# Row sums of one turn of an adjacency matrix: additions on GpSimd instead of sums on TensorE

## What is computed

```python
def _L0_gnn_ref(z, dist_matrix, W, B):
    msg = z @ W + B
    sens = exp(-(1.0 / r - 1.0 / MU) ** 2 / (2.0 * SIGMA * SIGMA))     # r = dist_matrix, MU 1, SIGMA 0.5
    weights = jnp.where(dist_matrix < CUTOFF, sens, 0.0)
    return weights @ msg

def _L1_gnn_ref(x, adj, W):
    A_hat = adj + jnp.eye(adj.shape[0], dtype=adj.dtype)
    d_inv_sqrt = jnp.sum(A_hat, axis=1) ** (-0.5)
    A_norm = d_inv_sqrt[:, None] * A_hat * d_inv_sqrt[None, :]
    support = x @ W.T
    return jax.nn.relu(A_norm @ support)

h = jnp.maximum(_layernorm(x, axis=-1), 0.0)
x = x + _L0_gnn_ref(h, adj, L0_gnn_W, L0_gnn_B)
h = jnp.maximum(_layernorm(x, axis=-1), 0.0)
x = x + _L1_gnn_ref(h, adj, L1_gnn_W)
```

## Time and profile before

| | |
|---|---|
| median of 3 runs | 580.74 us (579.77 to 583.24) |
| profiled execution | 580.75 us, its span 579.0 us |
| TensorE busy | 527.3 us (91%), granted clock 0.975 of full speed |
| DVE busy | 469.9 us (81%) |
| ACT busy | 462.3 us (80%) |
| GpSimd busy | 64.1 us (11%) |
| L443, the sums on TensorE | 256 instructions, 35.7 us |
| L697, the transposes on DVE | 64, 2303 ns each |
| L712, the cuts on DVE | 64, 2288 ns each |

### The profile page before, as it was taken

The page is one execution under the profiler, slowest core; times in us unless marked ns, Lnnn a source line. Parts: engine busy times, 40 slices in busy tenths (PEclk is TensorE's granted clock), DMA queues, the critical chain, the costliest instruction groups (busy, mean ns, idle before and its releaser), DMA issues.

```text
span 579.0 us, 4992 instructions
## 1 busy us (share of the span) xinstructions
PE 527.3 (91%) x1579; PEld 238.9 (41%) x1579; DVE 469.9 (81%) x556; ACT 462.3 (80%) x305; POOL 64.1 (11%) x100
## 2 busy tenths in 40 slices
PE   0658987989989999999999999999999999999995
PEld 0334423323333344344444444444444444445442
DVE  2999989999889896999999999995999559206244
ACT  1489999999899999898999989999699966920011
POOL 3993600000000000000000000000000001101000
PEclk9958998989999999999999999999999999999999
DMA  9999999999999997769979999998678040948223
GB/s 203 228 310 315 332 322 346 361 356 338 368 370 299 368 331 191 214 228 300 293 184 315 281 234 254 342 278 220 178 187 229 20 145 6 416 161 288 74 63 82
DMA packets 90652, 145.19 MB, mean 251 GB/s; under 512 B 10369, under 2 KB 81282, under 8 KB 81666
## 3 DMA queue, kind: packets, MB, share of 16 engines
q1 hardware_dynamic: 83088, 105.81, 64.8%
q0 software_dynamic: 5808, 38.28, 19.0%
q10 hardware_dynamic: 1730, 0.79, 0.7%
HBM read 106.04 MB, written 38.80 MB: 250 GB/s over the span
## 4 chain that ended last, share of the span: by engine, by line
PE 55%; ACT 26%; DVE 9%; issue 4%; DMA 3%; POOL 2%; ACTq 1%; DVEq 0%
PE acc L412 21%; PE mix L435 14%; PE mix L425 11%; ACT wt L568 7%; ACT wt L573 6%; ACT wt L587 5%; ACT wt L578 5%; DVE kept L697 3%; DMA x<-in_x_dram 3%; DVE rowpart L705 2%; PE mix L443 2%; PE acc L435 2%; POOL support L365 2%; DVE wt L712 2%; ACT wt L584 2%
## 5 line engine op out<-in xcount | busy, mean ns | idle before, releaser
L412 PE MATMUL acc<-wt,msg 128*128 128x512 f32 x512 | 237.5, 608 | 11.8 <-ACT wt L587 8.8
L412 PEld LDWEIGHTS acc<-wt,msg 128*128 128x128 f32 x512 | 96.0, 193 | 144.0 <-issue 118.4
L697 DVE STREAM_TRANSPOSE kept<-raw 128x2048 f32<-128x2048 f32 x64 | 147.4, 2303 | 2.5 <-DMA adj_t_spill<-kept 1.7
L712 DVE SCALAR_TENSOR_TENSOR wt<-kept 128x2048 f32<-128x2048 f32 x64 | 146.4, 2288 | 1.3
L568 ACT ACTIVATE wt<-wt 128x2048 f32<-128x2048 f32 x64 | 121.7, 1902 | 10.6 <-DVE wt L712 10.6
L573 ACT ACTIVATE wt<-wt 128x2048 f32<-128x2048 f32 x64 | 121.6, 1901 | 0.5
L425 PE MATMUL mix<-kept,support 128*128 128x512 f32 x224 | 101.1, 595 | 1.6 <-DVE kept L697 1.6
L587 ACT ACTIVATE wt<-wt 128x2048 f32<-128x2048 f32 x50 | 95.0, 1900 | 0.0
L578 ACT ACTIVATE wt<-wt 128x2048 f32<-128x2048 f32 x50 | 94.9, 1898 | 0.0
L435 PE MATMUL mix<-late,support 128*128 128x512 f32 x200 | 89.7, 593 | 0.0
L705 DVE TENSOR_REDUCE rowpart<-raw 128x16 f32<-128x4096 f32 x16 | 70.1, 4381 | 0.0
(11 more groups left out here) (93 smaller groups left out, 261.0 us busy)
## 6 DMA issues: line engine op xcount, KB each, us to landing
raw<-in_adj_dram SPq DMA_DIRECT2D x512, 128.0 KB, 6.2
adj_t_spill<-kept SPq DMA_DIRECT2D x35, 1024.0 KB, 10.6
late<-adj_t_spill POOLq DMA_DIRECT2D x26, 1024.0 KB, 8.6
raw<-adj_t_spill POOLq DMA_DIRECT2D x9, 1024.0 KB, 9.9
out_dram<-kept SPq DMA_DIRECT2D x30, 64.0 KB, 1.8
x<-in_x_dram POOLq DMA_DIRECT2D x24, 64.0 KB, 7.6
x<-in_x_dram ACTq DMA_DIRECT2D x8, 64.0 KB, 4.7
out_dram<-kept ACTq DMA_DIRECT2D x2, 64.0 KB, 2.1
```

What stands on the lines that cost most here:

```text
L412: mm = nc.tensor.matmul(acc0[:], msg[:, col(u) * T + k, :], wt[:, u % WTS, k, :], start=(first and k == 0), stop=(last and k == T - 1))
L697: nc.vector.transpose(dst, src).then_inc(turned, 1)
L712: nc.vector.scalar_tensor_tensor(out=wt[:, u % WTS], in0=v, scalar=CUTOFF, in1=v, op0=ALU.is_lt, op1=ALU.mult).then_inc(cut_done, 1)
```

## The change

In turn 3 TensorE no longer sums each unit. GpSimd adds the turned units up in `row_acc` (128x2048): the first addition takes units 24 and 25, each of the six others adds one more. TensorE sums the total with four products when all seven additions are done. `PE_SUMS` is 3 now, and `DVE_SUMS = 4` stands where `PE_SUMS` stood for the turns whose sums are DVE's. A transpose of the units 28 to 35 also waits for the addition that reads its slot. GpSimd's late loads are put between the additions by `load_unit`. For the 8 KB a partition that `row_acc` takes, the scratch of dynamic DMAs is set to 8192.

```diff
-PE_SUMS = 4
+PE_SUMS = 3
+DVE_SUMS = PE_SUMS + 1
+
+def added_by_pool(u):
+    return PE_SUMS <= u // G < DVE_SUMS
+
+def adds(u):
+    return max(1, u % G)

+def load_unit(j):
+    before = slot_before(j)
+    if before is None:
+        return G + 2 + j
+    return [u for u in sorted(JOBS) for _ in JOBS[u]][before] + 4

# GpSimd
+            def add(u):
+                pool.wait_ge(turned, u + 1)
+                if adds(u) >= 2:
+                    pool.wait_ge(pool_added, adds(u) - 1)
+                first = kept[:, (u - 1) % KEPT] if u % G == 1 else row_acc[:]
+                nc.gpsimd.tensor_tensor(row_acc[:].rearrange("p k i -> p (k i)"),
+                                        first.rearrange("p k i -> p (k i)"),
+                                        kept[:, u % KEPT].rearrange("p k i -> p (k i)"),
+                                        ALU.add).then_inc(pool_added, 1)
...
+            for u in range(G, UNITS):
+                for j in range(len(IN_TURN)):
+                    if load_unit(j) == u:
+                        load_late(j)
+                if added_by_pool(u) and u % G >= 1:
+                    add(u)
+            for j in range(len(IN_TURN), len(LOADED)):
+                load_late(j)

# TensorE
+            def sum_total():
+                pe.wait_ge(pool_added, G - 1)
+                for k in range(T):
+                    mm = nc.tensor.matmul(sum_bank[PE_SUMS][k * B:(k + 1) * B, :], ones[:], row_acc[:, k, :],
+                                          start=True, stop=True)
+                mm.then_inc(tiles_summed, 1)
...
                 if g >= 1 and idx < LAG:
                     multiply_weights(u - LAG)
-                if 1 <= g <= PE_SUMS and step_at(g, idx, "sum_quads"):
+                if u == DVE_SUMS * G:
+                    sum_total()
+                if 1 <= g <= DVE_SUMS and step_at(g, idx, "sum_quads"):
                     turn_sums(g - 1)

# ScalarE
-                act.wait_ge(tiles_summed, G * (g + 1))
+                act.wait_ge(tiles_summed, G * (g + 1) if g < PE_SUMS else G * PE_SUMS + 1)

# VectorE, in turn(u), with v = u - KEPT
+                    if added_by_pool(v):
+                        dve.wait_ge(pool_added, adds(v))

-    nc = _bacc.Bacc("TRN2", target_bir_lowering=False, num_devices=1)
+    nc = _bacc.Bacc("TRN2", target_bir_lowering=False, num_devices=1, dynamic_dma_scratch_size=8192)
```

More of the change, by code:

```diff
@@ L78 @@
 JOBS_FIRST = 4
-PE_SUMS = 4
+PE_SUMS = 3
[4 more added lines that the diff above has]
+    return max(1, u % G)
 def squared_by_dve(u):
-    return u < PE_SUMS * G and u % (4 if u < G else 2) == (3 if u < G else 1)
+    return u < DVE_SUMS * G and u % (4 if u < G else 2) == (3 if u < G else 1)
 STEPS = {"own_rows": (2, 3, 5), "copy_x1t": (1, 2, 6), "turn_x1": (2, 3, 5), "make_x1": (3, 4, 5),
@@ L167, in build @@
         wt = sb("wt", [P, WTS, T, ROWS])
+        row_acc = sb("row_acc", [P, T, ROWS])
         x1t = sb("x1t", [D, ROWS])
@@ L237, in build @@
         quad_done = sem("quad_done")
+        pool_added = sem("pool_added")
         tiles_summed = sem("tiles_summed")
@@ L296, in load @@
                 if n >= RAW:
-                    if n - RAW >= PE_SUMS * C4:
-                        sp.wait_ge(summed, n - RAW + 1 - PE_SUMS * C4)
+                    if n - RAW >= DVE_SUMS * C4:
+                        sp.wait_ge(summed, n - RAW + 1 - DVE_SUMS * C4)
                     sp.wait_ge(turned, 2 * (n - RAW + 1))
@@ L367, in _, with load_late @@
                 last.then_inc(h0_done, 1)
-            for j, (r, c) in enumerate(LOADED):
+            def add(u):
[7 more added lines that the diff above has]
+                                        ALU.add).then_inc(pool_added, 1)
+            def load_late(j):
+                r, c = LOADED[j]
                 slot = late_slot(j)
@@ L376, in _ @@
                     last_pair = max(n for n in range(PAIRS) if n % RAW == (slot - LATE) // 2)
[L377 removed]
+                    pool.wait_ge(summed, last_pair + 1 - DVE_SUMS * C4)
                     pool.wait_ge(turned, 2 * last_pair + 2)
@@ L454, in sum_quads @@
             def sum_quads(g):
-                pe.wait_ge(summed, C4 * (g + 1 - PE_SUMS))
-                if g == PE_SUMS:
+                pe.wait_ge(summed, C4 * (g + 1 - DVE_SUMS))
+                if g == DVE_SUMS:
                     pe.wait_ge(quad_stage, Q + 1)
@@ L493, in _ @@
                     multiply_msg(idx // 2)
-                if g > PE_SUMS and step_at(g, idx, "sum_quads"):
+                if g > DVE_SUMS and step_at(g, idx, "sum_quads"):
                     sum_quads(g - 1)
@@ L655, in _ @@
                     copy_h0((idx + 1) // 2)
-                if 1 <= g <= PE_SUMS and idx == 0:
+                if 1 <= g <= DVE_SUMS and idx == 0:
                     copy_sums(g - 1)
@@ L700, in row_sum @@
                 g, jp = n // C4, n % C4
-                if g >= PE_SUMS + 2 and jp == 0:
+                if g >= DVE_SUMS + 2 and jp == 0:
                     dve.wait_ge(quads_summed, g - 1)
@@ L768, in own_rows @@
                     dve.wait_ge(newton, 3 * g)
-                if g < PE_SUMS:
+                if g < DVE_SUMS:
                     nc.vector.tensor_copy(pows[:, 0, :], side[:, 0:T]).then_inc(rows_owned, 1)
@@ L798, in make_x1 @@
                 last.then_inc(hid_done, 1)
-                if g >= PE_SUMS:
-                    dve.wait_ge(rows_summed, g + 1 - PE_SUMS)
+                if g >= DVE_SUMS:
+                    dve.wait_ge(rows_summed, g + 1 - DVE_SUMS)
                 nc.vector.tensor_scalar(pows[:, 0, :], pows[:, 0, :], 1.0, None, ALU.add)
@@ L817, in turned_ahead @@
             def turned_ahead(u):
-                return u % 2 == 1 and u < PE_SUMS * G and squared_by_dve(u - 2)
+                return u % 2 == 1 and u < DVE_SUMS * G and squared_by_dve(u - 2)
             take_moments(0)
@@ L825, in _ @@
                     turn(u)
-                if g < PE_SUMS or u < PE_SUMS * G + 2:
+                if g < DVE_SUMS or u < DVE_SUMS * G + 2:
                     cut(u)
@@ L831, in _ @@
                         quad(u - 1)
-                if idx % 2 == 1 and g >= PE_SUMS:
+                if idx % 2 == 1 and g >= DVE_SUMS:
                     row_sum(u // 2)
@@ L841, in _ @@
                     make_support(g - 1)
-                if u >= PE_SUMS * G + 2:
+                if u >= DVE_SUMS * G + 2:
                     cut(u)
```

## The result

The changed kernel takes 596.18 us (median of 3 runs, 595.96 to 596.61) against 580.74 us before: ratio 1.0269, 95% interval 1.0245 to 1.0294, so 15.4 us slower. The forecast was 594.

What follows compares the result with a forecast made beforehand. DVE was taken as the chain up to 308 us, then TensorE. Additions of 4.5 us holding up DVE's two-operand passes sum to +13.6 us at T33: 580.75 + 13.6 = 594.4, 594 us; range 579 to 600.

Steps and rivals of the forecast that it cites:

- What bounds: DVE is the chain up to 308 us, then TensorE, so a shift of T33 is a shift of the end.
- T33: DVE's transpose of the unit numbered in the name, claimed to come at 260.6 instead of 247.00 us, +13.6.
- rival 4: Worse than 600 us, from additions above 5.5 us or a fall of TensorE's granted clock; chance 0.03.
- The additions' price: One GpSimd addition of 128x2048 float32 takes 4.5 us, between 3.9 and 5.5; seven are 31.5 us.
- Exclusion in both directions: Two-operand DVE passes and GpSimd's reads exclude each other; whichever holds the resource keeps it to the end of its instruction.
- Rivals 1 and 2: First: GpSimd yields to DVE, 580 us, chance 0.25. Second: additions hidden under transposes at no cost, 577.4 us, chance 0.08.
- Q23: DVE's square of unit 23, claimed to wait for the first addition and start at 192.7 instead of 188.76 us, +3.9.
- C29: DVE's cut of unit 29 in the fourth turn, claimed to be +10.7 us late.
- A29: GpSimd's addition for unit 29, claimed to run 231.7 to 236.2 us and hold small two-operand DVE passes behind C29.
- A31: GpSimd's addition for unit 31, claimed to hold DVE's cut of unit 32 to 256.2 instead of 241.47 us, +14.7.
- if GpSimd wins also between Q and C, +16: Case where GpSimd also gets in between DVE's square and cut: +16 us, 596.8 us.
- TensorE's gain, 3.3 us: Of 7.0 us of sums taken from TensorE, 3.3 us reach its product L478 and the DVE work behind it.

Runs made afterwards that it cites:

- e2: Changed kernel with all additions, DVE's cuts and squares of the fourth turn replaced by one-operand transposes of the same size: 577.62 us, ratio 0.9961 to the kernel before.
- e3: Changed kernel with each GpSimd addition replaced by three memsets, so GpSimd only writes: 578.19 us, ratio 0.9974 to the kernel before.
- e5: Changed kernel with each addition cut into four pieces of 512 columns: 584.41 us, ratio 1.0070 to the kernel before.
- e6: Changed kernel with each addition replaced by a GpSimd TENSOR_SCALAR reading one operand: 589.08 us, ratio 1.0144 to the kernel before.
- e4: Changed kernel with the additions kept and TensorE also summing each unit as before: 595.24 us, ratio 1.0266 to the kernel before.
- e9: Changed kernel with only the first three of seven additions, TensorE summing units 28 to 31 one by one: 584.48 us, ratio 1.0085 to the kernel before.
- e1: Changed kernel without GpSimd's additions, the total's buffer filled with ones once: 577.95 us, ratio 0.9969 to the kernel before.
- e7: Kernel before with only the scratch of dynamic DMAs set to 8192: 579.61 us, ratio 0.9985 to the kernel before.

## Why the prediction was right

**What bounds.** Right: DVE's T33 is 15.7 us late (262.39 against 247.00, and 0.3 for the axis) and the end is 15.4 us late. All of the loss arises between T25 and T33. TensorE's granted clock fell to 0.90 in the fourth turn, one of rival 4's conditions, but TensorE wasn't the chain there, and the time stayed under 600 us.

**The additions' price.** 4.54 us where 4.5 was taken, and 3.9 and 5.5 were the bounds. In e2, with nothing in the way, 4.55 to 4.58 us. The Trainium skill's 4.497 us for it (GPSIMD Engine Reference, Performance versus the Vector engine) is within 2% of that.

**Exclusion in both directions.** Right, and shown in both: the trace of after has DVE passes that wait for an addition and additions that wait for a DVE pass, e2 and e3 show that it takes DVE's two-operand passes (transposes of the same size aren't held) and GpSimd's reading, and e5 that the wait is as long as one instruction of the other side. Rivals 1 and 2 fall with Q23's 6.17 us. "To the end of the instruction" held for the additions, and not for e6's instruction.

**The sum.** Starts, with 0.3 us added for the axis of after:

| | forecast | measured |
|---|---|---|
| C25, behind Q23 | +3.9 | 194.56, +3.9 |
| C27 done, behind A27 | +8.6 | 214.4 against 206.7, +8.1 |
| C29's end | +10.7 | 235.1 against 221.1, +14.3 |
| T30 | +10.1 | 236.90, +9.2 |
| C31's end | +12.4 | 254.6 against 239.2, +15.7 |
| T33 | +13.6 | 262.39, +15.7 |

Up to T30 each term but C29's is within 0.9 us of the forecast. **One term was mis-sized**: A29 and A31. I had them start behind C29 and C31, and A31 half hidden beside T32. They got in between the square and the cut that follows it on DVE without a gap (C29 6.61 us, C31 6.60, each with a full 4.3 us of waiting in it). For A29 it made no difference, since it only changed which of DVE's passes waited. A31 was not beside a transpose at all: 3.3 us more at C31's end. C32, which I had held until 256.2, was then free of a hold, and the gap in front of Q31, which I had counted as gone, stayed (1.02 us). 15.7 against 13.6 is the whole error of the sum. The prediction had this order as the upper end of its own range ("if GpSimd wins also between Q and C, +16").

The total can be worked out in another way: DVE's passes are 23.0 us longer by the busy line, and it lost three waits, of 1.96, 0.19 and 5.10 us. 23.0 - 7.25 = 15.7 us. The same subtraction gives 15.8 for e4 (measured 15.4 by the ratio), 4.4 for e5, where 0.27 us of the first wait is left (4.1), 9.2 for e6 (8.4, with an interval from 5.7 to 11.0) and 5.5 for e9, where 3.09 of the 5.10 are left (4.9, from 3.0 to 6.9).

**TensorE's gain, 3.3 us.** Wrong in size, though the verdict didn't hang on it. The step that failed is "three of the five sums lie ahead of that product and give 1.3 us": I had looked at ACT's pass alone (it did come 1.4 us earlier in e1) and not at L466, which waits for DVE's L770. Before, L466 started 0.6 us behind L770's end (204.91 against 204.35), so it had little to gain. In e1 it stands for 2.6 us and the product behind it pays 1.35 us by its clock. The removal was worth 1.8 us.

**ACT and TensorE have time over, the kept slots, the late loads, the scratch.** Right: e4, e2 and e7.

## What to carry to other kernels

Work for an idle engine isn't free when its instructions and those of a busy engine exclude each other. Before moving adds to GpSimd, count DVE's instructions with two SBUF operands in the same stretch: here 32 us of additions (7 of 4.54) came beside 25 us of them (11 of 2.29), and DVE waited 23 us for them, for 1.8 us that the removal was worth. If GpSimd must read beside such passes, short instructions limit each wait to one of them (e5, a quarter of the cost). And a gain on an engine ends at its first wait for another: look at every wait between the removed work and the place where the gain is to be used.

## What had not been expected

- **The waiting side gets the interface next, even between two DVE instructions without a gap.** A29 and A31 had been waiting while Q27 and Q29 ran, and went ahead of C29 and C31. The sides alternate. With long instructions on both, each of the seven additions held one pass of DVE, four of them for 3.9 to 4.3 us and three, which ran in part beside a transpose, for 2.1.
- **Some small passes with one SBUF tensor are held too.** In e5 DVE's COPY of 128x4 took 1.21 us instead of 0.17 and a TENSOR_SCALAR of 128x128 1.32 instead of 0.28, both float32 from SBUF to SBUF. The 128x2048 transposes (all of e2's), BATCH_NORM_STATS2 of 128x128 (0.30 us at most) and the TENSOR_SCALAR L868 that reads PSUM were not held. With the change the additions didn't meet these, so this cost shows in e5 alone.
- **GpSimd's TENSOR_SCALAR of 128x2048 takes 5.37 us, longer than the addition's 4.54**, and lets DVE's pass go on after some 3.4 us.
- **A gap of 2.6 us on TensorE was followed by a product of 5.05 us instead of 3.70 (e1), one of 6.5 us by 6.17 us (e9).** Both times the granted clock in the stretch was below 1 (0.70 and 0.57). The length of the gap alone doesn't tell, though: in the changed kernel a product behind a gap of 2.5 us took 3.70 us and one behind 6.8 us took 5.14, and in e4 one behind 2.9 us took 3.70.
